# Post-norm attention and FFN block on one core: FFN weights turned to float by ScalarE in the projection instead of by GpSimd in attention, and another choice of the softmax sums that TensorE makes

## The reference

```python
def block(x):                      # x: (1, 4096, 512) float32
    q, k, v = split(x @ Wqkv, 3)
    q, k = layernorm_scale_only(q, q_ln_scale), layernorm_scale_only(k, k_ln_scale)
    scores = where(causal, -inf, (q / sqrt(32)) @ k.T)     # by head
    x = layernorm(x + (softmax(scores) @ v) @ out_W)
    Wg, Wu, Wd = ((w.astype(float32) - 128.0) * scale[:, None]
                  for w, scale in ((gate_w, gate_scale), (up_w, up_scale), (down_w, down_scale)))
    h = silu(x @ Wg.T) * (x @ Wu.T)
    return layernorm(x + h @ Wd.T)
```

## Time and profile before

| what | us |
|---|---|
| median of 3 runs | 2505.08 (2499.78 to 2505.93) |
| span of the profiled execution, first to last instruction | 2496.4 |
| TensorE matmuls busy | 2370.9 (95%) |
| VectorE busy | 1846.2 (74%) |
| ScalarE busy | 1291.2 (52%) |
| GpSimd busy | 610.2 (24%) |
| projection, 0 to 341 | 341 |
| attention, 341 to 1643 | 1302 |
| last stage, 1643 to 2496 | 853 |

### The profile page before, as it was taken

One profiled execution on the slowest core, in us unless ns is written; L12 is line 12 of the kernel. 1 busy time (PEld: TensorE's weight loads), 2 busy tenths in 40 slices (PEclk: granted clock), 3 DMA queues, 4 the chain that ended last, 5 costly groups with the idle time before them and its releaser, 6 DMA issues. The chain is left out here.

```text
span 2496.4 us, 38175 instructions
## 1 busy us (share of the span) xinstructions
PE 2370.9 (95%) x12610; PEld 1409.3 (56%) x12610; DVE 1846.2 (74%) x1765; ACT 1291.2 (52%) x1583; POOL 610.2 (24%) x410
## 2 busy tenths in 40 slices
PE   8999967999999999899999999969999999999997
PEld 6777732333333333333333333337888888888885
DVE  6555655999979999799997999973565565555654
ACT  3333335788888888778887788831111111111111
POOL 1111113633346333364331653300000000000000
PEclk9999968999999999999999999989999999999998
DMA  4444376110552105522036220054121110211100
GB/s 171 154 155 155 143 200 138 59 48 22 122 123 65 48 22 109 123 69 57 23 85 134 69 69 22 14 171 149 35 68 34 35 51 19 66 35 34 35 17 17
DMA packets 126432, 197.70 MB, mean 79 GB/s; under 512 B 14992, under 2 KB 39568, under 8 KB 126224
## 3 DMA queue, kind: packets, MB, share of 16 engines
q1 hardware_dynamic: 126224, 195.10, 27.7%
HBM read 122.70 MB, written 72.35 MB: 78 GB/s over the span
## 5 line engine op out<-in xcount | busy, mean ns | idle before, releaser
L905 ACT ACTIVATE probs<-score 128x1024 f32<-128x1024 f32 (+3 forms) x1152 | 1024.8, 956 | 253.2 <-PE score L822 229.6
L972 DVE TENSOR_TENSOR total<-total,probs 128x2048 f32<-128x2048 f32 (+3 forms) x464 | 1069.7, 2305 | 45.2 <-POOL probs L780 22.5
L822 PE MATMUL score<-qstk,kstk 98*128 98x512 f32 (+3 forms) x2304 | 664.1, 410 | 51.5 <-DMA kstk<-k_hi 19.0
L822 PEld LDWEIGHTS score<-qstk,kstk 98*128 98x128 f32 x2304 | 382.5, 191 | 547.2 <-ACT probs L905 436.5
L838 PE MATMUL ctx_acc<-probs,values 128*32 128x512 f32 (+3 forms) x4608 | 582.6, 578 | 19.5 <-POOL probs L780 19.5
L1309 ACT ACTIVATE hidden<-slot,gate_scale_sb 128x512 f32<-128x512 f32 x128 | 88.3, 690 | 625.0 <-PE slot L1238 625.0
L780 POOL TENSOR_SCALAR_AFFINE_SELECT probs<-probs 128x512 f32<-128x512 f32 x128 | 193.6, 1513 | 735.8 <-ACT probs L905 735.8
L1394 DVE SCALAR_TENSOR_TENSOR hidden<-slot,up_scale_sb,hidden 128x512 f32<-128x512 f32 x128 | 96.1, 750 | 261.8 <-ACT hidden L1309 261.8
L1180 POOL TENSOR_TENSOR rstd<-veps,minus_half 128x1 f32<-128x1 f32 x64 | 36.7, 574 | 803.9 <-DVE veps L1358 803.9
L838 PEld LDWEIGHTS ctx_acc<-probs,values 128*32 128x32 f32 x4608 | 91.7, 108 | 214.9 <-issue 179.5
L1238 PE MATMUL slot<-xt_hi,wg_sb 128*128 128x512 f32 x512 | 201.5, 394 | 5.2 <-issue 5.2
(11 more groups left out here) (102 smaller groups left out, 2198.9 us busy)
## 6 DMA issues: line engine op xcount, KB each, us to landing
qstk<-q_hi SPq DMA_DIRECT2D x64, 256.0 KB
kstk<-k_hi SPq DMA_DIRECT2D x64, 256.0 KB, 12.6
wq_int<-in_wq SPq DMA_DIRECT2D x48, 256.0 KB, 2.8
wq_float<-wq_f SPq DMA_DIRECT2D x48, 256.0 KB, 2.1
x_raw<-in_x_t SPq DMA_DIRECT2D x32, 256.0 KB, 3.5
v_rows<-v_out SPq DMA_DIRECT2D x32, 256.0 KB, 2.0
q_hi<-part_hi SPq DMA_DIRECT2D x32, 256.0 KB, 2.0
q_lo<-part_lo SPq DMA_DIRECT2D x32, 256.0 KB, 2.3
```

What stands on the lines that cost most here:

```text
L822: ins = pe.matmul(score[u % RING][:, i, cut(t):], kstk[0:ROWS, h, kb * P:(kb + 1) * P], qstk[0:ROWS, q_buffer[ch], h, cut(t):], start=True ...
L905: act.activation(probs[:, t % PB, 2 * p:2 * p + 2, cut(t):], score[u % RING][:, :, cut(t):], ACT.Exp).then_inc(exped, 1)
L972: dve.tensor_tensor(into, into, now, ALU.add).then_inc(added, 1)
```

## The change

The tiles of FFN weights are loaded, converted and stored in the projection: six tiles per chunk, one after every even unit. ScalarE converts (an activation Copy with bias -128, `turn_float`), SP loads and stores (`load_int`, `store_float`), and VectorE takes the largest absolute value of each row of a tile after every odd unit (`widest`) in place of the squares and their sum. GpSimd keeps only the masks in attention. `finish` compares the largest value with 4096 instead of the largest sum of squares with 4096 squared.

`by_pe` picks every tenth step from place 8 of a chunk on instead of every sixth from place 12 on. By the conditions these are places 12, 18, 24, 30 before (12 steps per group, in chunks 3 to 7) and places 10, 20, 30 after (10 steps per group, in chunks 2 to 7).

```diff
--- before.py
+++ after.py
@@ -73,6 +73,7 @@
     NU, NJ = 3 * ST, 2 * DC
+    WT = 3 * IC // NCH
     usual = [(st, m) for st in range(ST) for m in range(3)]
@@ -125,6 +126,9 @@
         zeros = sb("zeros", [P, 2 * HEADS * S // P])
+        wq_int = sb("wq_int", [P, 2, D], I32)
+        wq_f = sb("wq_f", [P, 2, D])
+        whole = keep["whole"]
@@ -178,9 +186,20 @@
             sp.dma_start(ow_raw[:], io["out_w"].rearrange("(g r) e -> r g e", r=P)).then_inc(ow_in, 16)
-            for s_, k in ((parts_stored, 32), (v_stored, 16)):
+            for s_, k in ((parts_stored, 32), (v_stored, 16), (wq_stored, 16)):
                 for one in s_:
                     sp.sem_inc(one, k)
+
+            def load_int(n, e):
+                sp.dma_start(wq_int[:, e % 2, :], io["wq"][bass.ds(n * WT + e, 1)].rearrange("a p x -> (a p) x"))\
+                  .then_inc(int_in[e % 2], 16)
+
+            def store_float(n, e):
+                sp.dma_start(dr["wq"][bass.ds(n * WT + e, 1)].rearrange("a p x -> (a p) x"), wq_f[:, e % 2, :])\
+                  .then_inc(wq_stored[e % 2], 16)
+
+            load_int(0, 0)
+            load_int(0, 1)
@@ -205,6 +224,13 @@
                                .then_inc(parts_stored[i % 4], 16)
+                    if u % 2 == 0:
+                        e = u // 2
+                        sp.wait_ge(floated, WT * n + e + 1)
+                        sp.nop(nofuse=True)
+                        store_float(n, e)
+                        if after or e + 2 < WT:
+                            load_int(n, e + 2)
@@ -352,6 +378,13 @@
+            def turn_float(n, e):
+                b = e % 2
+                act.wait_ge(int_in[b], 16 * (WT // 2) * n + 16 * (e // 2) + 16)
+                act.wait_ge(wq_stored[b], 16 * (WT // 2) * n + 16 * (e // 2) + 16)
+                act.wait_ge(whole_done, WT * n + e + 1)
+                act.activation(wq_f[:, b, :], wq_int[:, b, :], ACT.Copy, bias=-ZERO_POINT).then_inc(floated, 1)
+
             def body(n, c, par, before, after, half):
@@ -368,11 +401,14 @@
                         high(n if own else c, i)
+                    if u % 2 == 0:
+                        turn_float(n, u // 2)
...
         def _(dve):
+            dve.memset(whole[:], 0.0).then_inc(whole_done, 2)
             dve.memset(minus_half[:], -0.5)
@@ -431,6 +467,11 @@
                 dve.tensor_reduce(norm_max[:, i, bass.ds(o, 1)], norms[i][:], AX.X, ALU.max).then_inc(norms_read, 1)
+
+            def widest(n, e):
+
+                dve.wait_ge(floated, WT * n + e + 1)
+                dve.tensor_reduce(whole[:, bass.ds(n * WT + e, 1)], wq_f[:, e % 2, :], AX.X, ALU.max, apply_absolute_value=True).then_inc(whole_done, 1)
@@ -453,6 +494,8 @@
                             tops.append((n if own else c, i // DC, u + 3))
+                    if u % 2:
+                        widest(n, u // 2)
                 for t in tops:
@@ -504,12 +547,7 @@
         ch, kb = steps[t]
-        return not diagonal(t) and t - first[ch] >= ST * 3 and (t - first[ch]) % 6 == 0
-
-
-    WT = 3 * IC // NG
-    tiles_after = {ch: range(2 * (ch - 2), 2 * (ch - 1)) for ch in range(2, NCH)}
-    assert sum(map(len, tiles_after.values())) == WT
+        return not diagonal(t) and t - first[ch] >= ST * 2 and (t - first[ch]) % 10 == 0
@@ -676,19 +703,6 @@
                                  .rearrange("p b g d -> p b (g d)")).then_inc(v_in[j], 16)
-                def load_int(j):
-
-                    sp.wait_ge(floated, WT * g + j + 1)
-                    sp.nop(nofuse=True)
-                    sp.dma_start(wq_int[:, j % 2, :], io["wq"][bass.ds(g * WT + j, 1)].rearrange("a p x -> (a p) x"))\
-                      .then_inc(int_in[j % 2], 16)
-
-                def store_float(j):
-                    sp.wait_ge(floated, WT * g + j + 1 + 2)
-                    sp.nop(nofuse=True)
-                    sp.dma_start(dr["wq"][bass.ds(g * WT + j, 1)].rearrange("a p x -> (a p) x"), wq_f[:, j % 2, :])\
-                      .then_inc(wq_stored[j % 2], 16)
-
                 if before is None:
@@ -696,8 +710,6 @@
                 load("q", 1)
-                load_int(0)
-                load_int(1)
                 for j in range(1, NCH):
@@ -705,9 +717,6 @@
                     store(sp, g, ch - 2)
-                    for j in tiles_after.get(ch - 1, ()):
-                        store_float(j)
-                        load_int(j + 2)
@@ -718,16 +727,12 @@
                              .rearrange("g h u s -> (g h u) s"), flat_inv[:]).then_inc(inverse_stored, 16)
-                for j in tiles_after[NCH - 1]:
-                    store_float(j)
...
-            for b in range(2):
-                sp.wait_ge(wq_stored[b], 16 * (WT // 2) * NG + 16)
             sp.wait_ge(inverse_stored, 16 * NG + 16)
@@ -747,29 +752,6 @@
                             .then_inc(g_masked, 1)
-            pool.sem_inc(floated, 2)
-            pool.sem_inc(whole_done, 2)
-            for b in range(2):
-                pool.sem_inc(wq_stored[b], 16)
-            pool.wait_ge(whole_zero, 1)
-
-            def turn_float(g, j):
-
-                b = j % 2
-                pool.wait_ge(int_in[b], 16 * (WT // 2) * g + 16 * (j // 2) + 16)
-
-                pool.wait_ge(wq_stored[b], 16 * (WT // 2) * g + 16 * (j // 2) + 16)
-                pool.wait_ge(whole_done, WT * g + j + 1)
-                pool.nop(nofuse=True)
-                pool.tensor_scalar(wq_f[:, b, :], wq_int[:, b, :], -ZERO_POINT, None, ALU.add).then_inc(floated, 1)
-                pool.wait_ge(floated, WT * g + j + 1 + 2)
-                pool.wait_ge(whole_done, WT * g + j + 2)
-                pool.nop(nofuse=True)
-                pool.tensor_tensor(wq_square[:], wq_f[:, b, :], wq_f[:, b, :], ALU.mult).then_inc(wq_squared, 1)
-                pool.wait_ge(wq_squared, WT * g + j + 1)
-                pool.nop(nofuse=True)
-                pool.tensor_tensor(whole[:], whole[:], wq_square[:], ALU.add).then_inc(whole_done, 1)
-
             with pool.Fori(0, NG) as g:
@@ -779,9 +761,6 @@
                                            pattern=[[0, HG], [1, P]], channel_multiplier=-1).then_inc(masked, 1)
-                    if steps[t][1] == ST * steps[t][0] + ST - 1:
-                        for j in tiles_after.get(steps[t][0], ()):
-                            turn_float(g, j)
@@ -919,7 +898,6 @@
             dve.memset(ones[:], 1.0).then_inc(ones_ready, 1)
-            dve.memset(whole[:], 0.0).then_inc(whole_zero, 1)
             for j in range(NCH):
@@ -1128,6 +1106,8 @@
             sp.dma_start(down_scale[:], io["down_scale"].rearrange("(a h) -> a h", a=1).to_broadcast([P, D])).then_inc(small_in, 16)
+            for b in range(2):
+                sp.wait_ge(keep["wq_stored"][b], 16 * (3 * IC // 2) + 16)
             for i in range(2):
@@ -1329,7 +1309,7 @@
             dve.wait_ge(checked, 2)
-            dve.tensor_scalar(flag_f[:], check_top[:], WHOLE * WHOLE, None, ALU.is_gt).then_inc(checked, 1)
+            dve.tensor_scalar(flag_f[:], check_top[:], WHOLE, None, ALU.is_gt).then_inc(checked, 1)
             dve.wait_ge(checked, 3)
```

17 lines of the change are left out of this document (6 added, 11 removed).

## The result

The changed kernel takes **2469.66 us** (median of 4 runs, 2468.07 to 2476.69), beside 2505.51 for the kernel before (4 runs, 2499.78 to 2508.08): a ratio of 0.9868, 95% interval 0.9851 to 0.9884. Forecast were 2474.6 and a range of 2463 to 2492. The profiled execution took 2468.88 and spans 2467.1; a span of 2466 was forecast.

The account below looks back on a forecast made before the run. TensorE and its hand-over with ScalarE were taken to set the pace, VectorE's adds hidden behind them. Terms -6.8 - 21.8 - 2.6 + 0.7 = -30.5 us took 2505.1 to 2474.6 us, range 2463 to 2492.

Parts of the forecast that it names:

- Number of sums: Attention: TensorE's sums inside chunks go from 12 to 10 per group, eight fewer in the kernel, not 24 to 10.
- Sums, -6.8: Attention: eight fewer sums on TensorE save 0.85 us each, -6.8 us, ends -6 and -8.
- Adds hidden: Attention: VectorE's eight extra adds stay behind TensorE, and adds get shorter, near 2.29 us; cost 0.
- My balance: Long chunks: nine undisturbed VectorE adds between two sums take 20.9 us, while TensorE takes 22.2.
- the tipping point: Chunks 4 to 7: VectorE becomes the bound when an add with its gap takes more than 2.46 us.
- Chunk 3's stall, -21.8: Chunk 3 of each group: TensorE's four mask waits (14.3 us) and low clock after them (7.5) go; -21.8 us.
- Start of attention, -2.6: Start of attention: two integer tiles no longer queued ahead of the queries of chunk 2; -2.6 us, ends 0 and -5.
- Projection, 0, and +0.7 at its end: Projection: 48 conversions and 48 reductions are covered, cost 0; the last reduction adds +0.7 us, ends 0 and +1.4.
- The projection didn't pay: Rival, projection units: added work lands on TensorE's way, +63 us, 2538, chance 0.06; half, +31, 2505, chance 0.07.
- VectorE as the bound: Rival, chunks 4 to 7: adds staying at 2.82 us make VectorE the bound of attention; +84 us, 2559, chance 0.03.
- The stall didn't stay: Rival, chunk 3: its mask is late for a reason other than the weights, so the stall stays; 2496, chance 0.08.
- the fourth, "more goes": Rival, attention: the other mask waits shrink too, -5 us, and the clock holds; 2466 to 2468, inside the forecast's range.

Follow-up runs that it names:

- e2: Changed kernel with the old condition for TensorE's sums (12 per group), so only the weight work has moved; ratio 0.9855 to the kernel before.
- e1: Kernel before with only the new condition for TensorE's sums (10 per group), weight work still on GpSimd in attention; ratio 0.9995 to the kernel before.
- e7: Changed kernel with no sum on TensorE inside a chunk, VectorE making all adds; 2495.8 us, ratio 0.9969 to the kernel before.
- e3: Kernel before with no weight tile converted after chunk 2, two each after chunks 3 to 6, four after chunk 7; ratio 1.0023.
- e5: Kernel before with no weight tile after chunk 2, two after chunks 3 and 4, three after 5 and 6, two after 7; ratio 0.9926.
- e12: Kernel before, SP's queue reordered: last two tiles' stores and next group's first two integer loads behind its queries, keys and values; ratio 0.9969.
- e4: Kernel before with the first group's two integer tiles loaded behind the queries of chunk 2; ratio 0.9992 to the kernel before.
- e6: Changed kernel with the next group's loads held back in SP's queue until place 16 of chunk 7; 2480.9 us, ratio 0.9914 to the kernel before.
- e9: Changed kernel with each of the 48 weight-tile reductions in the projection done twice on VectorE; 2473.7 us, ratio 0.989 to the kernel before.
- e8: Changed kernel with the first group's queries of chunk 2 loaded behind keys and values of chunk 2, not 7; 2447.6 us, ratio 0.9784.

## Why the prediction was right, step by step

**Number of sums: right.** 320 matmuls for 384, as counted; not 24 to 10.

**Sums, -6.8: right in the rhythm, not seen in the time.** Steady shows 5.6 (e2 against after). Done alone it gave nothing in the time (e1): the rhythm gained 10.7 us, and the group starts lost 11.8, most of it where VectorE's last add and then TensorE's jump were late. I had costed the two halves as if they added up; the sums needed the weights gone.

**Adds hidden: right.** 2.291 us for every one, TensorE's wait for them 0.4 us. My balance (20.9 against 22.2) looked at stretches between two sums; e7 shows that the chunk's end is where it is settled. I had put the tipping point at 2.46 us for an add with its gap; e1, at 2.522 without the gap, is beyond it, and VectorE was late there, but at another place than I had said.

**Chunk 3's stall, -21.8: right.** e3 gives 22.7 and e5 18.5 in the steady part, e5 18.5 in the time (-13 to -24), so each near the forecast. Both the waits and the low clock went (62.69 of 63.00 us, 1.00), so adding the clock's share to the waits was right.

**Start of attention, -2.6: right, as far as the ledger shows.** The queries came at 402.10 for 405.17, though attention began 0.6 us later. The start takes 47.8 to 52.3 us in the five kernels with the integer tiles ahead of the queries (before, e1, e3, e5, e12) and 44.7 to 47.2 in the six without (after, e2, e4, e6, e7, e9). The time can't confirm it (e4).

**Projection, 0, and +0.7 at its end: right.** Units 3.7 us apart as before, a conversion at 0.630 us and a reduction at 0.677, share 0.68 for the 0.65 I had estimated. ScalarE reads integers at the price of floats; GpSimd's 3.53 was no neighbour of it. The check came 0.94 us later: 0.6 for the reduction ahead of `norm_max`, the rest from the last unit of chunk 7. The reason I gave for the 0 (0.15 us to spare in a unit) was too tight: e9 shows that twice the work on VectorE fits.

**The step that failed** is one sentence: "Later weight transfers of attention are hidden, and their going is worth nothing." Nobody waits for them, but they stood in SP's queue and on the DMA engines ahead of the next group's loads, and so in the way of the code that the engines fetch when they jump back. Reordering the queue alone was worth about 8 us (e12, 4 to 12), and ScalarE's two gaps went from 7.4 and 7.9 us to 3.6 and 3.7.

**How the sum comes out.** Between the two profiled spans lie 29.3 us: 25.5 in the steady part (the stall and the sums), 3.7 at the start of attention less 0.7 for its later beginning, 2.0 behind the last exponential, less 1.2 at the group starts. The 2.0 I hadn't foreseen: from the last exponential to the end it is 852.3 to 857.1 us in the six kernels that keep the weight work in attention and 850.4 to 851.2 in seven of the eight others (e7, with its late adds, has 861.2); what makes it isn't shown. The medians give 35.9, with an interval of 29 to 37. The forecast of 30.5 lies in it, so its 5 us from the median are no more than the noise allows. It is partly luck all the same: it had 6.8 for sums that are hardly seen in the time, and nothing for the jumps, and these two errors have opposite signs.

**The signs.** Attention, from its first exponential to its last, is 28 us shorter, a little less than the 29 to 31 that I had named; the others came as named: 40 sums, adds at 2.29, no wait for a mask above 1 us, units 3.7 us apart, the start 3 us shorter.

**The rivals.** The projection didn't pay (e9). VectorE as the bound is real, but needs fewer sums (e7) or GpSimd's work beside it (e1). The stall didn't stay. Of the fourth, "more goes", the reason was wrong: TensorE still waits 6.7 us for masks, where it had waited 5.2 beside the stall. What more went, went at the jumps and behind attention.

## What to carry to other kernels

Ask of a transfer not only who waits for it but what stands behind it: in the queue (e8, 22 us from one line's order) and on the DMA engines when an engine jumps to code that it hasn't got (e6, e12). When a producer is slightly slower than its consumer, look for the next point at which everything must have been handed over, since the lateness of many steps falls due there (e1, e7). And before moving work to another engine, see whether moving it within its own would do: half of this gain was to be had by one table (e5), but a careless version of that table lost it all again (e3).
